# Decoder layer on one core: q's ternary weights on ScalarE beside k's on VectorE, v's and the output projection's weights turned inside the attention's steps

## The reference, cut to what matters

```python
def _act_quant(x):
    s = 127.0 / jnp.clip(jnp.max(jnp.abs(x), axis=-1, keepdims=True), 1e-05)
    return jnp.clip(jnp.round(x * s), -128.0, 127.0) / s

def _weight_quant(w):
    s = 1.0 / jnp.clip(jnp.mean(jnp.abs(w)), 1e-05)
    return jnp.clip(jnp.round(w * s), -1.0, 1.0) / s

def _bitlinear(x, w):
    return jnp.einsum('bnc,oc->bno', _act_quant(x), _weight_quant(w))

qkv = _bitlinear(layernorm(x), w_qkv)       # w_qkv (1536, 512): q, k, v chunks of 512 rows
out = causal_softmax_attention(q, k, v)
x = x + _bitlinear(out, w_proj)             # w_proj (512, 512)
```

## Time and profile before

| | |
|---|---|
| median of 3 runs | 1492.63 us |
| all runs | 1494.4, 1491.86, 1492.63 us |
| span of the profiled execution | 1492.0 us |
| PE busy, share of the span | 1397.0 us, 94% |
| DVE busy | 1238.3 us, 83% |
| POOL busy | 1181.3 us, 79% |
| ACT busy | 867.5 us, 58% |

### The profile page before, as it was taken

One profiled execution on the slowest core, in us unless ns is written; L12 is line 12 of the kernel. 1 busy time (PEld: TensorE's weight loads), 2 busy tenths in 40 slices (PEclk: granted clock), 3 DMA queues, 4 the chain that ended last, 5 costly groups with the idle time before them and its releaser, 6 DMA issues.

```text
span 1492.0 us, 23946 instructions
## 1 busy us (share of the span) xinstructions
PE 1397.0 (94%) x8405; PEld 775.2 (52%) x8405; DVE 1238.3 (83%) x1965; ACT 867.5 (58%) x1433; POOL 1181.3 (79%) x903
## 2 busy tenths in 40 slices
...
DMA packets 171587, 133.57 MB, mean 90 GB/s; under 512 B 120500, under 2 KB 124748, under 8 KB 171468
## 3 DMA queue, kind: packets, MB, share of 16 engines
...
## 4 chain that ended last, share of the span: by engine, by line
PE 64%; DVE 12%; POOL 8%; ACT 7%; issue 7%; DMA 1%; POOLq 0%; SPq 0%; DVEq 0%; ACTq 0%
PE gu L788 20%; PE gu L802 10%; PE shared_bank L733 9%; PE y L755 3%; PE y L749 3%; PE y L752 3%; PE y L757 3%; PE y L758 3%; POOL pL L1696 3%; DVE blockmax L917 2%; DVE o_sb L957 1%; DVE z L1148 1%; ACT pH L1353 1%; DVE qkt L897 1%; ACT pT L1347 1%
## 5 line engine op out<-in xcount | busy, mean ns | idle before, releaser
L1576 ACT ACTIVATE shared<-shared_bank 128x512 f32<-128x512 f32 x162 | 96.2, 594 | 339.9 <-PE shared_bank L733 339.9
L1145 DVE TENSOR_TENSOR y<-shared,y 128x512 f32<-128x512 f32 x324 | 224.1, 692 | 46.4 <-ACT shared L1576 24.6
L1696 POOL TENSOR_TENSOR pL<-pT,pH 128x768 f16<-128x768 f32 x128 | 216.5, 1693 | 11.1 <-ACT pH L1353 4.9
L788 PE MATMUL gu<-fT,wu 128*128 128x512 f16 x768 | 183.0, 381 | 0.0
L1152 DVE TENSOR_REDUCE oT<-z 128x64 f32<-128x512 f32 x256 | 175.6, 686 | 8.8
L788 PE MATMUL gu<-fT,wg 128*128 128x512 f16 x768 | 181.4, 379 | 1.0 <-DMA fT<-fnl 1.0
L1148 DVE TENSOR_TENSOR z<-y,cT 128x512 f32<-128x512 f32 x236 | 162.4, 688 | 11.6 <-PE y L747 5.3
L1834 POOL TENSOR_TENSOR fuL<-fu,fuH 128x512 f16<-128x512 f32 x96 | 112.3, 1170 | 71.6 <-ACT fuH L1591 71.4
L802 PE MATMUL gu<-wd,fuH 128*128 128x512 f16 x384 | 145.8, 380 | 0.0
L802 PE MATMUL gu<-wd,fuL 128*128 128x512 f16 x384 | 145.6, 379 | 0.0
L1770 POOL TENSOR_TENSOR kv<-vT,cT 128x1024 f32<-128x1024 f32 x70 | 137.9, 1971 | 5.2 <-ACT vT L1531 5.2
...
## 6 DMA issues: line engine op xcount, KB each, us to landing
pack<-qkhl SPq DMA_DIRECT2D x256, 128.0 KB, 2.4
...
```

The lines of the kernel that those rows point to most:

```text
L788: made = T.matmul(bank[:], (wg, wu)[which][:, cb, ib * P:(ib + 1) * P], fT[:, cb, part, :], start=cb == 0 and part == 0, stop=cb == CB - 1 ...
L1145: chain.step(V.tensor_tensor(bank[:], shared[2 * part + half][:], bank[:], op))
L1696: G.tensor_tensor(pL[n % 2][:], pT[n % NP][:], pH[n % NP][:], ALU.subtract).then_inc(low_done, 1)
```

## The change

1. The magnitudes of w_qkv are added up by two engines: VectorE takes chunk 0 and half of chunk 2, ScalarE chunk 1 and the other half of chunk 2 (an Abs activation with an accumulator).
2. k's chunk is turned first, then q's. k is made ternary by VectorE alone (one more tensor_scalar in place of ScalarE's rounding). q is made ternary by ScalarE alone: the rounding, then a Sign activation with the bias -1.5 x 2^23. VectorE copies k's four turned blocks, ScalarE q's four. The projection goes q, k, q, k over the groups.
3. v's chunk is made ternary by VectorE (three passes) right after `scale_in(1)`, but is turned and copied in steps -3 to 0. w_proj is rounded and made ternary by ScalarE at step 2, and turned and copied at steps 3 to 5. Its scale is made by VectorE at step 0.
4. v of batch 0 is multiplied at steps 4 and 6 and split at 5 and 7. Piece 0 is worked on four steps later than before, at steps 6, 7, 8, 15 and 16. Pieces 1 to 15 stay.
5. GpSimd raises `power_in(0)` ahead of its last constants, and `power_in(1)` ahead of batch 0's `low_qk`. The turn of the scale rows ("tab") moves to the start. SP waits for chunk 1 before it issues x of batch 1. Some semaphores are merged.

```diff
+        FIRST_V_AT, FIRST_V_SPLIT_AT = (17, 19), (18, 20)
+        V_WEIGHTS_AT, PROJ_WEIGHTS_AT, LOAD_PIECES_AT = (-3, -1), (3, 4), 5
...
-            return n if k == 0 and 0 <= n < PIECES else None
+            return n if k == (0 if n else 4) and 0 <= n < PIECES else None
...
+        W_ORDER = (1, 0, 2, 3)
+        def wT_by_act(i, ob):
+            return i == 0 or (i >= 2 and ob % 2 == 0)
+        def turning(t):
+            for i, at in ((2, V_WEIGHTS_AT), (3, PROJ_WEIGHTS_AT)):
+                if t in at:
+                    yield i, range(2 * at.index(t), 2 * at.index(t) + 2)
+        def qk_groups(s):
+            return s % 2, 2 * (s // 2)
...
-            weight_total([0, 1, 2], 0)
-            turn_weights(0)
-            spread_c(0)
+            weight_total(0, 4, 0)
             for j in range(2):
                 turn_xq(0, j)
             turn_weights(1)
+            turn_weights(0)
+            spread_c(0)
             for g2 in range(4):
                 multiply_qk(0, g2)
-            weight_total([3], 1)
-            turn_weights(2)
-            turn_weights(3)
-            spread_c(1)
             for j in range(2):
                 turn_xq(1, j)
+            spread_c(1)
...
+                for i, blocks in turning(t):
+                    turn_weights(i, blocks)
+                if t == V_WEIGHTS_AT[-1]:
+                    weight_total(4, 1, 1)
...
             def ternary(i):
-                w.wait_ge(wround_done, i + 1)
+                w.wait_ge(wscale_done, 1)
+                w.wait_ge(wsum_act, 2)
+                chain.step(V.tensor_scalar(wraw[i][:], wraw[i][:], ws[:, 1:2], ROUND, ALU.mult, ALU.add))
+                chain.wait()
                 chain.step(V.tensor_scalar(wraw[i][:], wraw[i][:], ROUND - 1.0, ROUND + 1.0, ALU.max, ALU.min))
...
+            scale_qk(0, 0)
+            scale_qk(0, 1)
+            max_in(1)
+            scale_qk(0, 2)
+            scale_qk(0, 3)
+            scale_in(1)
             ternary(2)
-            max_in(1)
-            scale_in(1)
-            ternary(3)
+            magnitude(3, WB, 4)
...
+                for i, blocks in turning(t - 1):
+                    copy_weights(i, blocks)
+                if t == V_WEIGHTS_AT[-1] + 1:
+                    weight_scale(1, 1, 2, 1)
+                    w.wait_ge(wscale_done, 3)
+                    chain.step(V.tensor_tensor(ws[:, 5:6], ws[:, 0:1], ws[:, 2:3], ALU.mult))
...
+            def magnitude(i, first, col):
+                w.wait_ge(wraw_in[i], 16)
+                S.activation(tern[i - 1][:, first:WB, :], wraw[i][:, first:WB, :], ACT.Abs, accum_out=wsums[:, col:col + 1]).then_inc(wsum_act, 1)
+            def sign_weights(i):
+                w.wait_ge(act_step, 1 if i == 0 else 2)
...
+                S.activation(tern[i % 2][:], wraw[i][:], ACT.Sign, bias=minus_round[:]).then_inc(tern_act, 1)
...
+                if t == PROJ_WEIGHTS_AT[0] - 1:
+                    round_weights(3)
+                    sign_weights(3)
```

More of the change, by code:

```diff
@@ L322, in project_steps, with v_step @@
         def project_steps(t):
-            for b, k in batches(t, PROJECT_AT, PAIRS + 9):
+            for b, k in batches(t, PROJECT_AT, PAIRS + 13):
                 if b > 0 or k >= PAIRS:
                     yield b, k
+        def v_step(b, k, split):
+            at = (FIRST_V_SPLIT_AT if split else FIRST_V_AT) if b == 0 else (V_SPLIT_AT if split else V_AT)
+            return at.index(k) if k in at else None
         def halves(t):
@@ L497, in tensor_program, with turn_weights @@
             w = Waits(tensor)
-            def turn_weights(i):
-                for ob in range(WB):
-                    freed = (wT_act, 2 * i + ob // 2 + 1) if ob % 2 == 0 else (wT_dve, 2 * i + ob // 2 + 1)
+            def turn_weights(i, blocks=range(WB)):
+                for ob in blocks:
+                    by_act = wT_by_act(i, ob)
                     w.wait_ge(const_done, C_BASE)
-                    bank = misc1.take(("wT", i, ob), w, freed)[:].bitcast(BF16)
-                    w.wait_ge(tern_done, i + 1)
+                    bank = misc1.take(("wT", i, ob), w, (wT_act if by_act else wT_dve, wT_copies(i, ob, by_act)))[:].bitcast(BF16)
+                    if i in (1, 2):
+                        w.wait_ge(tern_dve, i)
+                    else:
+                        w.wait_ge(tern_act, 1 if i == 0 else 2)
                     for cb in range(CB):
@@ L872, in weight_scale @@
                 chain.wait()
-                chain.step(V.tensor_scalar(ws[:, at:at + 1], ws[:, at:at + 1], 1.0 / (n * C * C), EPS, ALU.mult, ALU.max))
+                chain.step(V.tensor_scalar(ws[:, at:at + 1], ws[:, at:at + 1], 1.0 / (chunks * C * C), EPS, ALU.mult, ALU.max))
                 chain.wait()
@@ L1319, in round_weights @@
[L1319 to L1326 removed]
+                w.wait_ge(wscale_done, 2 * use + 1)
@@ new lines, in copy_weights @@
+            def copy_weights(i, blocks=range(WB)):
+                dst, o_first = (wqkvT, i * C) if i < 3 else (wprojT, 0)
+                for ob in blocks:
+                    if wT_by_act(i, ob):
+                        w.wait_ge(wtr_pe, w_turned(i, ob))
+                        src = misc1.of["wT", i, ob][:].bitcast(BF16)[:, 0:CB * P].rearrange("p (c o) -> p c o", c=CB)
+                        S.activation(dst[:, :, o_first + ob * P:o_first + (ob + 1) * P], src, ACT.Copy).then_inc(wT_act, 1)
```

205 lines of the change are left out of this document (103 added, 102 removed).

## The result

The changed kernel takes **1506.38 us** (median of 4 runs, 1505.78 to 1507.36) against 1493.26 us (4 runs) for the kernel before: a ratio of 1.0088, 95% interval 1.0074 to 1.0102. It is slower by 13.1 us. The forecast was slower by 8.9 us, with a range that ended at 1505.5. The direction was right, the size was not. Further down, one execution of `four_edits` (1518.67 us) and one of the kernel before (1665.7 us) ran at a lower granted clock (0.94 and 0.84), and the ratios leave them out.

The account below looks back on a forecast made before the run. No engine bounds the whole span: a chain to the pack, then VectorE, ScalarE with GpSimd close, GpSimd from 109 to 147 us. Terms -2.3 - 1.1 + 4.6 + 4.8 + 3.1 = +9.1 gave 1501.5 us, range 1492.0 to 1505.5.

Parts of the forecast that it names:

- (d): Steps 1 to 8: moved VectorE work fills steps 4 to 7, ScalarE's w_proj work may hold the turn; +4.8 us.
- (a): GpSimd's last two low_qk held until v's ternary passes end at 36.3; pack starts at about 38.7: -2.3 us.
- (b): x of batch 2 still behind the pack's 16 DMAs; batch 2's statistics start at 52.9: a further -1.1 us.
- The prologue: Before the first projection: scale at about 16.6, projection of batch 0 at about 26.3 instead of 32.41, 6.1 us earlier.
- rival 1: The port holds nobody: GpSimd runs low_qk between or beside VectorE's passes, pack at 34.9; 1497.7 us, chance 0.15.
- (c): Batch 2's statistics to first take_max: third group waits for a scaling, TensorE at low clock; 14.2 us, +4.6.
- rival 5: Slower still: low clock lasts into the score steps and ScalarE's 3.9 us hold the scores; +12, 1504.5 us, chance 0.08.
- (e): Piece 0's two GpSimd operations move from steps 11, 12 to 15, 16, where GpSimd has little idle time: +3.1 us.
- Rivals 2 and 3: Piece 0 costs GpSimd nothing: about 1498.4, chance 0.12; that plus no port hold: 1494.6, no change, chance 0.10.
- The faster rival: Pack at 34.9, moved work falls into idle time, prologue's -6.1 reaches the end: 1486.5 us, chance 0.10.
- the signs that would have shown the prediction wrong: Pack before 36 us, steps 1 to 3 under 1.8 each, or GpSimd idle over 2 between steps 16 and 24.

Follow-up runs that it names:

- four_edits: Changed kernel with x of batches 2, 3 before the pack, w_proj's sum before v's passes, piece 0 back on GpSimd's earlier steps, w_proj's rounding and Sign at step 0: 1487.26 us.
- busy_steps: Changed kernel with 35 added matmuls, results never read, in TensorE's waits at steps 0, 2, 3 and 7: 1503.14 us.
- sum_first: Changed kernel with w_proj's magnitude sum on VectorE ahead of v's three ternary passes: 1505.28 us.
- x_first: Changed kernel with x of batches 2 and 3 issued ahead of the first pack's 16 DMAs on SyncE's queue: 1494.05 us.
- busy_groups: Changed kernel with 74 added matmuls in TensorE's waits around the first blocks of v, none in the steps: 1505.3 us.
- v_turn_late: Changed kernel with v's chunk turned at steps -1 and 0 instead of -3 and -1: 1502.51 us.
- sign_step0: Changed kernel with w_proj's rounding and Sign on ScalarE at step 0 instead of step 2: 1503.74 us.
- six_busy: four_edits with v's chunk turned at steps -1 and 0, batch 0's v multiplied at 1, 3, split at 2, 4, plus 23 matmuls in TensorE's waits: 1491.65 us.

## Why the prediction was right or wrong

The step that failed is term (d). It was mis-sized, since the sum priced the score steps at TensorE's upper clock, and it had nothing from `take_max(8)` to (12). The runs showed the clock at the lower level in both places: +8.4 us up to `take_max(12)`, where the sum had +4.8, and +4.1 when added matmuls held the clock up (`busy_steps`). A further fall of the clock, at 434 us, was not in the sum at all. The other misses are smaller and partly cancel: (a) and (b) together came out 1.9 us better than forecast, and all the rest 6.3 worse. That the sum is off by 4.4 us only (13.5 for 9.1) is in part luck. Two slips in its arithmetic are small: 1501.1 and 0.6 are 1501.7, not 1501.5, and the pieces named in (c) add up to 14.1, not 14.2.

**The prologue** was right: the scale at 16.4, the projection at 25.84. The Sign pass, priced like the rounding at 1.94, took 1.99.

**(a) The port** was wrong in how the hold works. I let GpSimd wait for all three passes, as one row had it, and the pack start at 38.7. It started at 36.03. GpSimd and VectorE took turns: two passes of 2.06 instead of 1.23, and four `low_qk` in 6.47 instead of 4.51. The conflict costs 1.9 us (`sum_first`), where my sum had 3.8. So rival 1, a port that holds nobody, is out too. The Trainium skill, page "SBUF — State Buffer", section "Who interferes with whom", says that whichever of the two starts first has the port pair for that one instruction. The 2.06 us passes agree, and the alternation is what I had named and set aside. Who goes next when one instruction ends is not settled here: in the earlier trace rows a short GpSimd operation ended only with the second of VectorE's two passes.

**(b)** had the chain right: the statistics followed the pack, at 50.99 and not 52.9. From the pack to the statistics it is 14.96 us, and 15.31 before, so the term itself is -0.35 and not -1.1: the queue took 10.86 us instead of 10.45, and x of batch 2 4.0 us to land instead of 3.7. That x stands behind the pack was worth far more than the sum said: `x_first` took 12.3 us off. I had seen the chain, and priced it only as a shift.

**(c)** was right in kind, +5.4 for +4.6. With this order the low clock costs 2.5 (`busy_groups`). The old order alone, at the low clock, undoes nearly the whole (`v_turn_late`, 4.9).

**(d)** is the term that was mis-sized: +6.8 instead of +4.8 up to `take_max(8)`, beyond its upper bound of 6, and +1.6 more up to (12), where I had nothing. Its VectorE part stood in kind: +4.5 from (4) to (8), nearly the same with the clock held (+4.3). With the clock held the whole of (0) to (8) is +4.1 (23.18 against 19.08), which is close to the 4.8. ScalarE's hold is 1.3. One reading under it was wrong: VectorE had been busy for 17.4 of the 19.1 us before, not 18.8. The steps that took the work in were full (10.5 of 11.0 us), the early ones were not. What the sum left out is the clock in these steps. I priced steps 1 to 8 with durations of rows at the full rate, and put the low clock in the score steps into the last rival alone, at 0.08. It was there: 0.50 from 66 to 79 us and 0.57 at 90 to 94. Held up, it gives 2.1 us from (0) to (3), 0.5 to (4) and 1.6 from (8) to (12). So rival 5 came true in part beside the forecast's own terms, and its 1504.5 is the nearest to the measured time. The Trainium skill, page "TensorE: Matmul & The Clock Gate", section "Part 1: The HAM clock gate", says that the clock follows how busy the engine has been of late. `busy_steps` is that rule as an experiment, and the trace agrees: 1.00 where it was 0.50.

**(e)** was right to 0.1 us: 3.05 measured, 3.06 given back. Rivals 2 and 3 are out.

**Not foreseen at all** is the fall of the clock at about 434 us, 1.6 us. It is in the traces of the changed kernel and of ten of its fourteen variants, and not in those of `sign_step0`, `v_turn_late`, `six_busy` and `busy_groups`, nor in the two of the old program. The same wait of 1.38 us stands there in all of these traces, with the fall and without it. What decides it stays open, and no run was made for it. Each trace is one execution, so how much of the medians it explains is not known.

**The faster rival** asked for a first `take_max` before 62.9. `x_first` meets that condition by far, with 54.62, and is still no faster than before: the part behind that `take_max` is 11.8 us longer, by (d), (e) and the falls of the clock. So the first `take_max` did not decide it alone.

Of the signs that would have shown the prediction wrong none came, if narrowly: the pack started at 36.03 (the limit was 36), steps 1 to 3 took 2.3 to 2.8 us each, and GpSimd was idle for 0.1 us from 112 to 143. None of them asked for the clock in the steps.
